# Fused cross-attention and FFN: fill, expansion front and contraction reordered, six blocks of h held, loads of h begun by ScalarE

## The reference, cut to what matters

```
x    = x + attention(layernorm(x), ctx) @ Wo.T     # x: 4 x 2048 x 512, 16 heads of 32, 77 keys per batch
xq   = fake_quant(layernorm(x), clip_x)            # scale = sigmoid(clip) * max|all of it| / 127, rounded, clipped
gate = xq @ quant(w_gate).T ; up = xq @ quant(w_up).T        # 1408 inner columns, scale per row of w
h    = fake_quant(silu(gate) * up, clip_down)      # scale from max|h| over ALL tokens
out  = x + h @ quant(w_down).T
```

## Time and profile before

| | |
|---|---|
| median of three runs | 1153.25 us |
| the profiled execution | 1156.43 us |
| its span (first to last instruction) | 1154.6 us |
| attend, expand, contract (from the timeline) | 0 to 658, 658 to 977, 977 to 1155 us |
| PE busy in the span | 1096.4 us (95%) |
| DVE, ACT, POOL busy | 764.8, 619.8, 403.0 us |
| granted PE clock, mean | 0.979 of full |
| DMA | 223.18 MB, 193 GB/s over the span |

### The profile page before, as it was taken

The page is one execution under the profiler, slowest core; times in us unless marked ns, Lnnn a source line. Parts: engine busy times, 40 slices in busy tenths (PEclk is TensorE's granted clock), DMA queues, the critical chain, the costliest instruction groups (busy, mean ns, idle before and its releaser), DMA issues. The chain is left out here.

```text
span 1154.6 us, 17335 instructions
## 1 busy us (share of the span) xinstructions
PE 1096.4 (95%) x6142; PEld 616.8 (53%) x6142; DVE 764.8 (66%) x1383; ACT 619.8 (54%) x760; POOL 403.0 (35%) x321
## 2 busy tenths in 40 slices
PE   8689999999999999999999799999999997899898
PEld 5555666666666666666665444444444443344333
DVE  6445777677767666665554667777777777675665
ACT  4246556555555546555445257565656563755350
POOL 5355444455444544444331000000000000456678
PEclk9899999999999999999999989999999999899999
DMA  6333776568655576456436446767676522999977
GB/s 238 98 52 83 189 200 181 122 187 225 162 131 141 187 183 157 112 160 146 66 109 209 142 147 239 233 233 237 233 240 225 164 33 78 388 413 417 424 286 262
DMA packets 149535, 223.18 MB, mean 193 GB/s; under 512 B 67920, under 2 KB 76752, under 8 KB 143568
## 3 DMA queue, kind: packets, MB, share of 16 engines
q1 hardware_dynamic: 149456, 222.16, 61.9%
HBM read 137.41 MB, written 72.52 MB: 182 GB/s over the span
## 5 line engine op out<-in xcount | busy, mean ns | idle before, releaser
L1052 POOL TENSOR_TENSOR c_y<-x,c_y 128x512 f32<-128x512 f32 x64 | 112.4, 1785 | 395.2 <-DVE c_y L1086 377.5
L716 PE MATMUL a_Q<-a_xT,wq 128*128 128x512 f32 x768 | 197.1, 407 | 11.0 <-DVE a_q L615 11.0
L974 PE MATMUL e_G<-e_cT,gu 128*128 128x512 bf16 x704 | 181.8, 381 | 1.1 <-ACT e_cT L897 1.1
L883 ACT ACTIVATE e_sg<-e_G,x_gus 128x512 f32<-128x512 f32 x176 | 119.0, 685 | 117.1 <-PE e_G L974 117.1
L978 PE MATMUL e_U<-e_cT,gu 128*128 128x512 bf16 x704 | 181.7, 381 | 0.0
L938 DVE SCALAR_TENSOR_TENSOR h<-e_U,x_gus,e_sg 128x512 f32<-128x512 f32 x176 | 131.8, 749 | 72.7 <-PE e_U L978 47.3
L751 PE MATMUL a_O<-a_wo,a_aT 128*128 128x512 f32 x720 | 176.5, 394 | 0.0
L716 PEld LDWEIGHTS a_Q<-a_xT,wq 128*128 128x128 f32 x768 | 142.4, 192 | 63.8 <-issue 35.8
L1124 PE MATMUL c_Y<-dn,gu 128*128 128x512 bf16 x704 | 156.6, 386 | 14.3 <-DVE gu L1079 14.3
L419 POOL TENSOR_TENSOR a_aT<-a_att,a_aT 128x512 fp32r<-128x512 f32 x64 | 82.5, 1290 | 212.1 <-ACT a_aT L492 212.1
L515 ACT ACTIVATE a_qT<-a_q 128x512 fp32r<-128x512 f32 x64 | 40.4, 632 | 208.9 <-DVE a_q L615 203.4
(11 more groups left out here) (127 smaller groups left out, 1234.5 us busy)
## 6 DMA issues: line engine op xcount, KB each, us to landing
x<-x_d SPq DMA_DIRECT2D x32, 1024.0 KB, 7.1
h_d<-h SPq DMA_DIRECT2D x24, 1024.0 KB, 4.1
h<-h_d SPq DMA_DIRECT2D x11, 1536.0 KB, 18.0
a_xr<-in_x SPq DMA_DIRECT2D x64, 256.0 KB, 3.9
a_xt<-in_xT SPq DMA_DIRECT2D x64, 256.0 KB, 4.8
x_d<-a_xr SPq DMA_DIRECT2D x64, 256.0 KB, 3.5
a_xs<-in_x SPq DMA_DIRECT2D x60, 256.0 KB, 4.8
out<-c_y SPq DMA_DIRECT2D x15, 1024.0 KB, 10.4
```

The costliest lines, as they stand in the source:

```text
L716: mm = nc.tensor.matmul(Q[:], wq[:, wp, j, P * n.g:P * (n.g + 1)], xT[:, n.par, xp, j], start=(ins == 0), stop=(ins == 3 * KT - 1))
L883: nc.scalar.activation(sg[:, s], G[:, t % GU], ACT.Silu, scale=gus[:, t:t + 1]).then_inc(silued, 1)
L974: mm = nc.tensor.matmul(G[:, t % GU], gu[:, t, k], cT[:, p, k], start=(k == 0), stop=(k == KT - 1))
L1052: nc.gpsimd.tensor_tensor(y[:, p, t], x1[:, p, t], y[:, p, t], ALU.add).then_inc(added, 1)
```

## The change

What it does, by stage:

- Tokens are laid out as p*4 + t instead of t*128 + p in a block: `x1_d` becomes [block, partition, tile, 512], so a load of `x1` and a store of the output has one 8 KB piece per partition; a tile's load from x (`xs`, `xr`) and its store to `x1_d` has 2 KB pieces 8 KB apart in memory.
- attend: `rsb` of block 1 is made as for block 0, by four transposes on PE in slot 0 and a DVE copy, without the round trip through memory. DVE scales `Q` before it reduces `mx`, in all slots. The four stores of `dsc` are spread over slots 56 to 59; the load of `dscale` is in slot 62.
- expand: the chain of small operations is shorter (no copy of the maximum to 128 columns, three fused operations for four, the multipliers of block 0 released first); `cT` of block 0 is copied in four parts, and PE's first matmuls wait part by part. Blocks 10 to 15 stay on chip (`HELD_FROM = 11`); blocks 0 to 9 are stored.
- contract: ACT itself issues the loads of h (10 blocks). `x1` becomes a ring of four blocks, the sum is formed in it and stored from it; `y` is a ring of two tiles. Block 0 is coded and cast in six pieces (1, 1, 2, 2, 2, 3 tiles) and multiplied tile by tile over the four banks. The last block's sum is on DVE instead of POOL.

```diff
-HELD_FROM = 12
+HELD_FROM = 11
 ...
-    x1_d = dram("x1_d", [BLOCKS, TT, P, D], F32)
+    x1_d = dram("x1_d", [BLOCKS, P, TT, D], F32)
-    x_t = x.rearrange("b (n t p) d -> (b n) t p d", t=TT, p=P)
+    x_t = x.rearrange("b (n p t) d -> (b n) t p d", t=TT, p=P)
 # attend, SP
-                    if k == W_FIRST + WSTEPS + 5:
-                        sp.wait_ge(w_scaled, 2 * IT + KT)
-                        for r in range(KT):
-                            sp.dma_start(dsc_d[r], dsc[:, r:r + 1]).then_inc(ds_out, 16)
-                    if k == W_FIRST + WSTEPS + 7:
+                    row = k - (W_FIRST + WSTEPS + 6)
+                    if 0 <= row < KT:
+                        sp.wait_ge(w_scaled, 2 * IT + row + 1)
+                        sp.dma_start(dsc_d[row], dsc[:, row:row + 1]).then_inc(ds_out, 16)
+                    if k == W_FIRST + WSTEPS + 12:
-                    if k % 4 == 2 and (n := at(k, 6)) and n.block > 0:
+                    if k % 4 == 2 and (n := at(k, 6)) and n.block > 1:
 # attend, DVE: moved from behind the reduction of mx to ahead of it
+                    if (n := at(k, 4)):
+                        dve.wait_ge(q_done, n.n + 1)
+                        after(dve, qT_l, n.n)
+                        if n.n == TT:
+                            dve.wait_ge(r_turned, 2)
+                            dve.wait_ge(q_scaled, TT)
+                            nc.vector.tensor_copy(rsb[:], A[:]).then_inc(rsb_rdy, 1)
+                            dve.wait_ge(rsb_rdy, 2)
+                        if n.block > 1:
+                            dve.wait_ge(rsb_in, 16 * (n.block - 1))
+                        nc.vector.tensor_tensor(q32[:], Q[:], rsb[:], ALU.mult).then_inc(q_scaled, 1)
 # attend, PE
+                    if k == 0:
+                        turn_rs(1)
 # expand, DVE
-                nc.vector.tensor_copy(tall[:], tmax[:].to_broadcast([P, P])).then_inc(s_tmax, 1)
+                nc.vector.tensor_reduce(tmax[:], hi[:], AX.X, ALU.max).then_inc(s_tmax, 1)
 ...
+                own.step(nc.vector.reciprocal(inv[:], gmax[:]))
+                for a, z in ((0, TT), (TT, TILES)):
+                    own.step(nc.vector.tensor_scalar(xmul[:, a:z], rs[:, a:z], inv[:, 0:1], None, ALU.mult))
+                    nc.vector.scalar_tensor_tensor(out=xadd[:, a:z], in0=mean[:, a:z], scalar=-1.0, in1=xmul[:, a:z],
+                                                   op0=ALU.mult, op1=ALU.mult).then_inc(s_scale, 1)
 # contract
+        FIRST_CH = ((0, 1), (1, 2), (2, 4), (4, 6), (6, 8), (8, IT))
+        def ring(k):
+            return x1[:, k % 4] if k % 4 < 2 else z[:, k % 4 - 2]
 # contract, SP
+                load_x1(2)
+                load_x1(3)
+                for k in range(BLOCKS + 1):
                     if k >= 2:
+                        sp.wait_ge(added, (k - 1) * TT)
+                        sp.dma_start(out_t[ORDER[k - 2]], ring(k - 2)).then_inc(y_out[(k - 2) % 4], 16)
+                    if 3 <= k < LAST:
+                        sp.wait_ge(y_out[(k - 3) % 4], 16 * ((k - 3) // 4 + 1))
+                        load_x1(k + 1)
 # contract, ACT
+                def load_h(k, n):
+                    a, e = CH[n]
+                    act.wait_ge(coded, upto(k, e))
+                    nc.scalar.dma_start(h[:, BUFFER[k], a:e].rearrange("p t n -> p (t n)"),
+                                        h_d[ORDER[k + NH], :, TOK * a:TOK * e]).then_inc(h_in[n][k % NH], 16)
 # contract, DVE
+                        after(dve, added, min(i - 1, LAST * TT), 1 << 30)
+                        dve.wait_ge(downed, i + 1)
+                        nc.vector.tensor_tensor(y[:, i % 2], Y[:, TT * (k % 2) + t], dns[:], ALU.mult).then_inc(scaled, 1)
+                        if k == LAST:
+                            ...
+                            nc.vector.tensor_tensor(ring(k)[:, t], ring(k)[:, t], y[:, i % 2], ALU.add).then_inc(last_added, 1)
 # contract, PE: block 0
+                for j in range(IT):
+                    pe.wait_ge(cast, upto(0, max(hi for lo, hi in FIRST_CH if lo <= j)))
+                    for t in range(TT):
+                        mm = nc.tensor.matmul(Y[:, t], cb[:, 0, j, P * t:P * (t + 1)], dn[:, :, j],
+                                              start=(j == 0), stop=(j == IT - 1))
```

More of the change, by code:

```diff
@@ L896, in _ @@
                 act.wait_ge(first_turned, TT)
-                nc.scalar.activation(cT[:, 0, 2:4], T[:, 1].rearrange("p (a n) -> p a n", a=2), ACT.Copy).then_inc(first_rdy, 1)
+                for k in (1, 3):
+                    nc.scalar.activation(cT[:, 0, k], T[:, k % 2, TOK * (k // 2):TOK * (k // 2 + 1)], ACT.Copy).then_inc(first_odd, 1)
                 run(act, blk)
@@ L1008, in contract, with pieces, upto @@
         h_in = [[sem(f"c_h_in{n}{b}") for b in range(NH)] for n in range(2)]
-        x1_in = [sem(f"c_x1_in{p}") for p in range(2)]
-        y_out = [sem(f"c_y_out{p}") for p in range(2)]
-        coded, cast, downed, scaled, added = (sem("c_" + n) for n in ("coded", "cast", "downed", "scaled", "added"))
-        CH = ((0, 6), (6, IT))
-        LAST = BLOCKS // 2
+        x1_in = [sem(f"c_x1_in{r}") for r in range(4)]
+        y_out = [sem(f"c_y_out{r}") for r in range(4)]
+        last_out = sem("c_last_out")
+        coded, cast, downed, scaled, added, last_added = (sem("c_" + n) for n in (
+            "coded", "cast", "downed", "scaled", "added", "last_added"))
+        CH = ((0, 6), (6, IT))
+        FIRST_CH = ((0, 1), (1, 2), (2, 4), (4, 6), (6, 8), (8, IT))
+        LAST = BLOCKS - 1
+        def pieces(k):
+            return FIRST_CH if k == 0 else CH
+        def upto(k, tile):
+            return sum(len(pieces(b)) for b in range(k)) + sum(hi <= tile for _, hi in pieces(k))
+        def ring(k):
+            return x1[:, k % 4] if k % 4 < 2 else z[:, k % 4 - 2]
         with nc.Block() as block:
@@ L1045, in _ @@
             def _(pool):
-                def add(u, p):
-                    k = 2 * u + p
-                    if not isinstance(u, int) or u > 0:
-                        pool.wait_ge(x1_in[p], 16 * u)
+                for k in range(LAST):
+                    residual_in(pool, k)
                     for t in range(TT):
-                        pool.wait_ge(scaled, k * TT + t + 1)
-                        nc.gpsimd.tensor_tensor(y[:, p, t], x1[:, p, t], y[:, p, t], ALU.add).then_inc(added, 1)
@@ L1065, in _ @@
                     if k >= 2:
-                        act.wait_ge(cast, (k - 1) * len(CH))
-                    for n, (lo, hi) in enumerate(CH):
+                        act.wait_ge(cast, upto(k - 2, IT))
+                    n = 0
+                    for lo, hi in pieces(k):
                         if k >= NH:
-                            act.wait_ge(h_in[n][k % NH], 16 * (k // NH))
+                            act.wait_ge(h_in[CH.index((lo, hi))][k % NH], 16 * (k // NH))
                         nc.scalar.activation(c8[:, k % 2, lo:hi], h[:, BUFFER[k], lo:hi], ACT.Copy, scale=hinv[:, 0:1]).then_inc(coded, 1)
+                        if k < BLOCKS - NH and lo >= CH[n][1]:
+                            load_h(k, n)
+                            n += 1
@@ L1072, in _, with to_bf16 @@
+                    if k < BLOCKS - NH:
+                        load_h(k, n)
             @block.vector
             def _(dve):
-                def to_bf16(u, p):
-                    k = 2 * u + p
+                own = Chain(dve, s_own)
+                def to_bf16(k):
                     after(dve, downed, (k - 1) * TT, 1 << 30)
-                    for n, (lo, hi) in enumerate(CH):
-                        dve.wait_ge(coded, k * len(CH) + n + 1)
-                        nc.vector.tensor_copy(cb[:, p, lo:hi], c8[:, p, lo:hi]).then_inc(cast, 1)
@@ L1081, in scale @@
-                def scale(u, p):
-                    k = 2 * u + p
-                    after(dve, y_out[p], 16 * u, 1 << 30)
-                    for t in range(TT):
-                        dve.wait_ge(downed, k * TT + t + 1)
-                        nc.vector.tensor_tensor(y[:, p, t], Y[:, TT * p + t], dns[:], ALU.mult).then_inc(scaled, 1)
-                own = Chain(dve, s_own)
+                    for lo, hi in pieces(k):
+                        dve.wait_ge(coded, upto(k, hi))
+                        nc.vector.tensor_copy(cb[:, k % 2, lo:hi], c8[:, k % 2, lo:hi]).then_inc(cast, 1)
```

196 lines of the change are left out of this document (91 added, 105 removed).

## The result

The changed kernel takes 1141.53 us (median of 4 runs, 1140.24 to 1144.84) beside 1153.47 for the kernel before on the same chip (1152.59 to 1154.49): ratio 0.990, 95% interval 0.988 to 0.992. That is a gain of 12 us where 25.7 were forecast; it lies in the range (1119 to 1142), 14 us above the predicted time. Read along the spans, each stretch in us, with the forecast beside it. In this table, and wherever a slot is named without k, slots are counted from the first multiplication by the reciprocal denominators: slot 0 is k = 3, the first slots of a block are 1, 5, 9 and so on, the third ones 3, 7, 11.

What follows compares the result with a forecast made beforehand. PE bounds most of the kernel, with stalls in the fill, expand's front and contract (DMA-bound in its middle). Sum: 9.0 - 1.5 + 1.4 + 1.7 + 5.8 + 0.2 + 7.6 + 1.5 = 25.7 us, so 1127.6 us; range 1119 to 1142.

Steps and rivals of the forecast that it cites:

- Fill: Start of attend, 24 to 95 us: scaling first lets projections start sooner; 9.0 us gained, bounds 2.0 to 11.
- Rival D: Fill: its wait is replaced by one for loads of x; gain 2 instead of 9, 1135 us; chance 12%.
- Steady slots of attend: Attend after the fill: the later reduction costs 1.5 us through waits for rsb; bounds nothing to 5 us lost.
- rival E: Attend: reduction behind scaling sets the pace, kernel slower; 0.5 us in 60 slots costs 30 us, 1158; chance 4%.
- Stores of dsc: Late attend: stores no longer stand ahead of the last rsb load; 1.4 us gained, bounds 0 to 2.
- Front of expand: Start of expand: fewer small operations and part-wise copies bring PE's first matmul sooner; 1.7 us gained, bounds 1.0 to 2.2.
- Contract: Last stage: head 5.8, removed copy 0.2, middle 7.6 and tail 1.5 us gained; 15.1 in the stretch table.
- tail: From PE's end to the span's end: 5.7 us falls to 4.2; gain 1.5 us, bounds 0 to 2.5.
- Late loads: Middle of contract: 1.5 us taken off the 9.1 us gain for a load that comes late; bounds 0 and 12.
- Rival B: Contract: queues share DMA by row packets, h 58%, x1/output 178 GB/s, x1 some 12 us late; 1140 us; chance 18%.
- Rival C: Contract: issuing loads of h holds ACT up, 8.5 us per block, 22 us late; 1150 us; chance 8%.
- The signs named ahead: Fill, attend, expand and contract: marks to tell outcomes apart, such as 16 contract blocks in about 154 us.

Runs made afterwards that it cites:

- mx_first: Changed kernel with DVE's reduction of mx again ahead of the scaling of Q from k = 2 on: 1128.55 us, 0.979 of the kernel before.
- mx_first2: Second run of the changed kernel with the reduction ahead of the scaling from k = 2 on, on another comparison's chip: 0.977 of the kernel before.
- attend_old: Changed kernel with attend's whole slot program as before (order, round trip for block 1, dsc stores together), new token layout kept: 1137.05 us, 0.986 of before.
- rows4k: Reduction-first version of the changed kernel, with contract's loads of h cut to two tiles each (4 KB rows, 60 loads): 1137.38 us, 0.987 of before.
- rows6k: Reduction-first version of the changed kernel, with contract's loads of h each cut in two (about three tiles, 40 loads): 1130.44 us, 0.979 of before.

## Why the prediction was wrong

**Fill: right, its exact size by luck.** 9.0 us forecast and measured, with both projections within 0.6 us of their places. But the other profiled executions with the new fill reach the mark at 61.3 to 65.0 us, which would be 8 to 12 us gained. Rival D (a load of x in the wait's place) did not come: the next projections waited 0 and 1.04 us.

**Steady slots of attend: the step that failed,** the price of putting the scaling first. It was -1.5 us in the forecast, -5 as the bound, and came out as -12.7 in the profile and -13 by mx_first. The working looked at one late slot near 305 us, where 1.42 us of slack take up 0.68, and carried it to all. At 305 us the slots of both kernels do take the same 9.2 us. The loss is all in the first 22 slots, the ones in which the 22 row tiles of `w_gate` and `w_up` pass through DVE, ACT, POOL and SP's queue (that these take the slack was not tested). Against mx_first, slots 0 to 4 lose 6.7 us, 13 to 16 lose 3.3, slot 21 loses 2.3 and the others 1.0 together; the 32 slots behind give 1.0 back. The fill's part had named the place without its price: the stall of 2.4 us from the round trip of block 2 was to stay, but with the reduction behind the wait for `rsb` it became 5.48 us. The working priced a wait for `rsb` at its excess over the slack, once, and no more. What it left out: the matmuls at the lower clock level around the waits (5.1 us in one pair of executions, 1.7 in the other), the factors held up by POOL in the third slot, and a second way to PE: ACT takes its work in order and waited up to 4.2 us for DVE's `w_inv` (41.0 us from 60 to 275 us, 10.2 in mx_first2), so the exponentials came late and PE waited 3.08 us for one at 104.41. This second way is small in sum: PE's waits for exponentials from 60 to 275 us are 3.6 us, 3.1 in mx_first. The whole is rival E's mechanism, but in a part of the slots: it was priced per slot over 60 and given 4%, where one stretch with less slack than the rest was enough.

**Stores of dsc:** 1.4 forecast, and the stretch shows 5.2, of which attend_old, with the old stores, has 4.4 as well. No gain of this edit is shown.

**Front of expand:** 1.1 of 1.7, at its lower bound; the first gate matmul comes 6.7 us after the maximum of DVE L936 ends, where 5.0 were named. **Contract:** 12.9 of 15.1. PE started 5.6 us sooner (5.8), block 0 took 12.6 us and not 11.6 (the granted clock is 0.5 until 982.8), the fifteen others 144.9 us and not 144.0, the tail fell from 5.7 to 4.2 as forecast. Late loads were priced at 1.5 us and cost 2.4 (144.9 less 142.5).

**Rival B:** its rate was right, its price not. While h is loaded, an issue of `x1` comes every 11.65 us (1050.51, 1062.15, 1073.77, 1085.41), 2.1 MB each, 180 GB/s: 0.42 of 429 GB/s, as 8 KB are of 8 and 11. The forecast had 178 for B, and 12 us late (its own rates give about 10: 7.9 pairs of 2.3 us, less 8). But PE lost 2.4 us: POOL waited, and the pairs in the ring covered the rest. Smaller rows on either side shift the share as rows say they should: h lands twice as fast against 2 KB pieces, `x1` comes in 7.7 to 8.7 us against 4 KB rows. The Trainium skill (DMA: Bandwidth & Descriptors, "Queues, rings and completion order") says that a DMA engine goes round between its queues a whole packet at a time; by the shares of this case the trace agrees, if a packet is a row. The DMA view counts 2880 packets on ACT's queue for the 20 loads of h, which have 2560 rows: a packet there is a row, but for 16 others a load. That the engines take turns by these packets is shown by the shares alone.

**Rival C:** refuted here (0.33 us for each issue); its hold-up of ACT, though not its price, shows in rows4k and rows6k.

The signs named ahead: POOL's waits for `x1` of over 3 us (5.2 and 5.4) told of B. Contract's PE took 157.3 us where 154 was named, its first matmul 1.4 us behind ACT's first piece and not 1.2. The two signs that were to refute the prediction (contract's PE over 160 us, the fill under 5) didn't come; neither looked at attend. PE's waits for `mx` after 95 us came to 3.2 us, under the 5 that were to clear E. That sign was too narrow: it left out the stretch before 95 us, the waits for ACT, and matmuls that run slow without a listed wait.

That the measured time lies in the stated range, by 0.5 us, is luck: the slow end was set by rival B, whose late loads cost PE 2.4 us here, and not by the order in attend.

## What to carry to other kernels

Where an operation is put ahead of another on a shared engine, look at the waits of the one that moves ahead: they now stand before everything behind it, and slack read in a late slot need not hold in an early one. Beside the wait itself, price matmuls at the lower clock level around it (here 2 to 5 us beside 7.5 us of waiting), and look at what the other engines now run at the same time. Where two queues share the DMA engines, the size of their rows sets their shares; smaller rows on one side give the other more, but in the runs with 40 and 60 loads the issuing engine was then held up.

## What was not expected of the hardware

A DVE operation on 128x4 took 1.21 us and not 0.16 when POOL's operation on 128x512 (1.29 us) had begun just ahead of it, and ended with it; the mean of 16 was 1.08. The first of the four did the same at 61.78 (0.78 us, POOL's from 61.26 for 1.28). Not every operation does: DVE's aggregation at 192.66 kept its 0.18 us beside POOL's operation of 191.84 to 193.14. Why, no run here shows. Issues of loads by ACT, 0.33 us each with 20 loads of 128 rows, took up to 6.5 us with 60 and 7.5 with 40, from near 1004 us on, when 30 and 24 had been issued. As the time is the same in both, the number of loads is not shown to be the cause. The load of `rsb`, which waits for the factors' stores, was issued 9 to 13 us after the first of them, with four stores of 0.5 KB or with one of 2 KB; other transfers of SP were in flight beside them. The DMA share in attend rose from .65 to .84 with pieces of 2 KB read 8 KB apart, at the same GB/s, and no time was lost by it.
